# A recommendation ranker on one core: the gathered rows of a tile in groups of 4, 3, 3, 3 chunks instead of 4, 3, 4, 2

## The reference

```python
x0 = emb[ids].reshape(B, -1)
x = x0
for i in range(3):
    x = x0 * (x @ cross_w[i])[:, None] + cross_b[i] + x
h = relu(x0 @ w1 + b1)            # 1664 -> 1024
h = relu(h @ w2 + b2)             # 1024 -> 512
h = relu(h @ w3 + b3)             # 512 -> 256
y = sigmoid(concat([x, h], 1) @ out_w + out_b)
```

## Time and profile before

| | us |
|---|---|
| median of 3 runs | 531.18 |
| the profiled execution | 530.56 |
| its span, first to last instruction | 528.8 |
| PE matmul busy | 480.8 (91%) |
| POOL busy | 379.6 (72%) |
| DVE busy | 186.4 (35%) |
| ACT busy | 84.7 (16%), its DMA issues not counted |

### The profile page before, as it was taken

The page is one execution under the profiler, slowest core; times in us unless marked ns, Lnnn a source line. Parts: engine busy times, 40 slices in busy tenths (PEclk is TensorE's granted clock), DMA queues, the critical chain, the costliest instruction groups (busy, mean ns, idle before and its releaser), DMA issues.

```text
span 528.8 us, 11324 instructions
## 1 busy us (share of the span) xinstructions
PE 480.8 (91%) x2912; PEld 442.2 (84%) x2912; DVE 186.4 (35%) x391; ACT 84.7 (16%) x159; POOL 379.6 (72%) x407
## 2 busy tenths in 40 slices
PE   2699899899999989899898989999899898999997
PEld 1399698898989889798887988888898888989996
DVE  5766414232142423224242321424232142423325
ACT  4642111111011111102011110101111010101111
POOL 5777776777777777777777777777777777777720
PEclk9999999999999999999999999999999999999999
DMA  7971111111111111111111111111111111111100
GB/s 234 387 263 29 28 29 27 28 29 27 29 29 29 28 28 30 29 29 29 27 29 26 30 27 30 26 30 29 26 30 25 30 27 28 27 28 28 28 10 2
DMA packets 19700, 24.90 MB, mean 47 GB/s; under 512 B 9305, under 2 KB 10292, under 8 KB 19636
## 3 DMA queue, kind: packets, MB, share of 16 engines
q0 software_dynamic: 12800, 13.13, 11.2%
q1 hardware_dynamic: 4770, 10.74, 5.7%
q10 hardware_dynamic: 2066, 0.31, 0.3%
HBM read 24.41 MB, written 0.01 MB: 46 GB/s over the span
## 4 chain that ended last, share of the span: by engine, by line
PE 55%; POOL 14%; issue 10%; ACTq 9%; DMA 5%; DVE 4%; ACT 3%; POOLq 0%; DVEq 0%
PE l_bank L717 41%; POOL x_raw L347 14%; ACTq L387 8%; DMA x_raw<-in_L_rec_emb,idx 4%; PE x_bank L717 4%; PE x_bank L729 4%; PE h_bank L771 3%; ACT xT_hi L400 2%; DVE x_raw L516 2%; ACTq L384 1%; PE l_bank L802 1%; DVE xT_lo L523 1%; PE h_bank L741 1%; DVE h2T_lo L528 1%; ACT h2T_hi L411 1%
## 5 line engine op out<-in xcount | busy, mean ns | idle before, releaser
L347 POOL DMA_INDIRECT x_raw<-in_L_rec_emb,idx x400 | 378.8, 947 | 125.5 <-issue 107.7
L717 PE MATMUL l_bank<-w_hi,xT_hi 128*128 128x342 f32 (+1 forms) x624 | 144.9, 333 | 3.5 <-DVE xT_lo L523 3.3
L717 PE MATMUL l_bank<-w_lo,xT_hi 128*128 128x342 f32 (+1 forms) x624 | 137.9, 321 | 0.0
L717 PE MATMUL l_bank<-w_hi,xT_lo 128*128 128x342 f32 (+1 forms) x624 | 137.7, 321 | 0.0
L717 PEld LDWEIGHTS l_bank<-w_hi,xT_hi 128*128 128x128 f32 x624 | 104.0, 191 | 7.9 <-DVE xT_lo L523 5.6
L717 PEld LDWEIGHTS l_bank<-w_lo,xT_hi 128*128 128x128 f32 x624 | 106.8, 191 | 0.0
L717 PEld LDWEIGHTS l_bank<-w_hi,xT_lo 128*128 128x128 f32 x624 | 106.3, 190 | 0.0
L523 DVE TENSOR_TENSOR xT_lo<-x_bank,xT_hi 128x512 fp32r<-128x512 f32 (+1 forms) x66 | 38.2, 578 | 158.5 <-ACT xT_hi L400 158.5
L400 ACT ACTIVATE xT_hi<-x_bank 128x512 fp32r<-128x512 f32 (+1 forms) x66 | 33.5, 507 | 270.3 <-PE x_bank L729 220.4
L729 PE MATMUL x_bank<-identity,x_raw 128*128 128x128 f32 x208 | 34.7, 279 | 27.0 <-DVE x_raw L516 27.0
L729 PEld LDWEIGHTS x_bank<-identity,x_raw 128*128 128x128 f32 x208 | 25.0, 142 | 36.7 <-issue 31.0
(11 more groups left out here) (94 smaller groups left out, 296.5 us busy)
## 6 DMA issues: line engine op xcount, KB each, us to landing
ids<-in_L_rec_emb SPq DMA_DIRECT2D x1152, 0.2 KB
ids<-in_L_rec_emb ACTq DMA_DIRECT2D x896, 0.2 KB
w_raw<-in_L_rec_w SPq DMA_DIRECT2D x18, 512.0 KB, 15.0
x_raw<-in_L_rec_emb,idx POOLq DMA_INDIRECT x400, 2.4
b_rows<-in_L_rec_b SPq DMA_DIRECT2D x1, 512.0 KB
b_rows<-in_L_rec_b SPq DMA_DIRECT2D x1, 256.0 KB
ids<-in_r_ids SPq DMA_DIRECT2D x1, 208.0 KB, 2.7
b_rows<-in_L_rec_b SPq DMA_DIRECT2D x1, 128.0 KB
```

The costliest lines, as they stand in the source:

```text
L347: pool.indirect_dma_start(out=dst, out_offset=None, in_=emb, in_offset=rows).then_inc(landed, 16)
L717: done = pe.matmul(bank[:, 0:b - a], x[:, k, :], w[:, k, a:b], start=(k == 0 and n == 0), stop=(k == last_k and n == 2))
```

## The change

Groups 2 and 3 of tiles 0 to 14 become chunks 7 to 9 and 10 to 12.

```diff
-    SIZES = [4, 3, 4, 2]
+    SIZES = [4, 3, 3, 3]
```

## The result

The changed kernel takes 539.26 us (538.27 to 539.73, 4 runs) against 531.19 us: a ratio of 1.0154, 95% interval 1.0134 to 1.0175. That is slower by 8.1 us where 3.9 were forecast, and outside the range that ended at 537.5. The profiled execution took 539.73 us, its span 537.9.

What follows compares the result with a forecast made beforehand. POOL's gathers and ACT's queue were taken to set PE's pace. Tile 0 +3.3, tile 1 +0.1, tiles 2 to 13 +0.1 and tile 14 +0.4 sum to +3.9 us: median 535.1 us, range 532.6 to 537.5.

Steps and rivals of the forecast that it cites:

- What bounds the kernel: Whole kernel: POOL's gathers and ACT's queue set PE's pace; whatever delays PE up to T(2, 0) delays POOL for good.
- Tile 0, +3.3: Tile 0: PE waits for DVE's splits before T(0, 3) and chunk 10, +3.46 us, less 0.12 for T(0, 2).
- Tiles 1 to 14, +0.6: Later tiles: +0.1 us in tile 1, +0.1 in tiles 2 to 13 together, +0.4 in tile 14.
- Chunks 10 to 12 take 3 x 1.42 = 4.26: Each later tile: the three chunks behind the new wait run at 1.42 us each, 4.26 us.
- 12.13 - 0.11: Tiles 2 to 13: time from x_hi of group 1 to group 3, 12.13 us before, 0.11 less with 384 columns.
- the 5.70 of T(13, 2): Tile 13 before the change: four chunks behind the wait took 5.70 us, read as still 1.42 each.
- The gathers: Late tiles: POOL, 3.4 us late from tile 2 on, and ACT bind about together at the end.
- POOL instead of ACT: Late tiles: ACT's issuing costs less than read, PE catches up with POOL; median 533.4 us, chance 0.15.
- The slow clock: Tile 0: the two chunks behind the waits take 2.17 us, not 1.42; +1.5 more, 536.6 us, chance 0.05.
- Not slower: Tile 0 costs nothing, so POOL isn't delayed and late tiles gain; 530.4 us, chance 0.10.

Runs made afterwards that it cites:

- e1: Changed kernel with make_whole(0, 3) moved up to after split 14 and x_lo(0, 3) to after split 15: 534.88 us, ratio 1.0083.
- e9: Changed kernel with ACT's shares 8, 12, 4, 12, 12, 16, DVE's places in tile 0 left as they are: 530.87 us, ratio 1.0019.
- e6: e1 with four of ACT's DMAs taken from the fetch ahead of x_hi(t, 2), shares 8, 12, 4, 12, 12, 16: 527.18 us, ratio 0.9940.
- e5: e1 with four of ACT's DMAs moved from the fetch ahead of x_hi(t, 3) to the one behind it: 529.15 us, ratio 0.9973.
- e2: Changed kernel with ACT's shares 11, 12, 4, 13, 10, 14 instead of 8, 12, 4, 16, 12, 12: 607.04 us, ratio 1.1415.
- e11: e6 with shares 8, 12, 4, 14, 10, 16, two of them no multiples of four: 543.91 us in its one run.
- e4: Kernel before the change with ACT's shares 11, 12, 4, 13, 10, 14: 604.80 us, ratio 1.1389.
- e10: Changed kernel with only make_whole(0, 3) moved up to after split 14, x_lo(0, 3) still after split 16: 537.31 us, ratio 1.0136.
- e3: e1 with ACT's shares 11, 12, 4, 13, 10, 14: 603.50 us, ratio 1.1359.
- e8: e1 with the transposes of group 3 put back behind chunk 8 in tiles 1 to 13: 534.83 us, ratio 1.0070.

## Why the prediction was right and wrong

- *What bounds the kernel: right.* POOL and ACT's queue are the two, and whatever holds T(2, 0) holds POOL: 4.6 us late in the changed kernel, 0.4 in e1.
- *Tile 0, +3.3: right in mechanism, a little short.* `make_whole` to transposes took 0.72 and `x_lo` to PE 0.60, as was said, and the waits were 1.73 and 1.62. Two small terms were mis-sized: three transposes after a wait take 0.52, not 0.33 (45.93 to 46.45), and the chunk behind the second wait takes 1.69, not 1.42. The stretch lost 3.9 us where the sum had 3.46. T(0, 2) gave back 0.26, not 0.12, so that tile 0 lost some 3.7 us. In the runs DVE's places are worth 3.8 to 4.2 us: the ratios of the changed kernel and e1 differ by 0.0071, those of e9 and e6 by 0.0079.
- *Tiles 1 to 14, +0.6: wrong, and this is the step that failed.* e1 puts them at 4.7 us. The mechanism was right: the gathers' wait goes, ACT's takes its place, and the wait before chunk 10 is there in every tile. The terms that were mis-sized are "Chunks 10 to 12 take 3 x 1.42 = 4.26" (they take 4.51) and "12.13 - 0.11" for the two fetches (12.08 measured, mean of twelve). Per tile that is 0.25 + 0.06 = 0.31: 30.96 forecast, 31.27 measured. So the slower start of PE behind a wait was put at nothing. Fourteen tiles at 0.25 make 3.5 us, twelve at 0.06 make 0.7, and with the 0.6 of the forecast that gives 4.8. The price of the restart stood in the rows of before: the two chunks behind a wait took 3.10, not 2.84. The prediction took the opposite from the 5.70 of T(13, 2), but there the three transposes stand between the wait and the chunks and bear the price themselves, 0.52 instead of 0.33. The same price, paid at chunk 7, is why PE waits 0.46 us before chunk 10 and not 0.7.
- *The gathers: right that they don't hold the late tiles, by more than forecast.* POOL and ACT were to bind about together at the end. But a tile takes 31.27 us, no less than POOL's 31.25, so PE never catches up with POOL, and now and then POOL waits for PE instead. It is 6.0 us late at field 24 of tile 13 (449.56 against 443.56), not 3.4. The low rival, "POOL instead of ACT", is what e5 and e6 made happen by easing ACT's queue.
- *The slow clock.* It came in the profiled execution, 1.6 us on half of layer 2 (4.61 against 3.04), at a place that the rival didn't name. The Trainium skill (TensorE: Matmul & The Clock Gate, "What's actually happening") has the clock fall when TensorE idles. The trace agrees as to the fall (0.51 from 60 to 62 us), and e9, with the same waits and 3.06, shows that it need not come.
- *"Not slower": wrong, and its condition wasn't enough.* It asked only that tile 0 cost nothing, and gave 530.4. e1 met that (its tile 0 ends 0.2 us earlier than before the change) and took 534.88, because ACT's part stayed. e6 removed both.

## What to carry to other kernels

When a group is resized, look for every list elsewhere that was laid out for the old sizes: here two numbers in DVE's order of splits, and the places where ACT issues DMAs. The groups alone made the kernel 1.5% slower; with both fitted to them it is 0.6% faster than before. A wait that comes back in every tile has to be priced with the slower start behind it, and a row of the same instructions right behind a wait gives that price.

## What the runs showed of the hardware

- A register load on ACT's queue is slow when it doesn't start at a multiple of four in its row: 4, 10, 12 and 14 registers took 1.17, 2.42, 2.88 and 3.30 us (e2, e11), where 4, 8, 12 and 16 from such a start took 0.56, 0.73, 0.96 and 1.20 in the kernel before. With four such loads in a tile the kernel was 14% slower (e2 to e4). The Trainium skill (DMA: Bandwidth & Descriptors, "Latency and other measured facts") gives a floor of some 600 ns for such a load and says that the compiler unrolls it by four; the trace agrees roughly: the shortest load of the kernel before, of four registers, took 486 ns, somewhat under that floor, and four registers more added some 0.2 us.
- The first chunk of nine matmuls behind a wait took 1.69 us instead of 1.42, behind a wait of 1.62 us (tile 0); behind one of 0.40 (tile 8), three chunks took 4.51 instead of 4.26, nearly the same price.
- Leaving out the last 2 us of the span, the granted clock fell once in the traces of the changed kernel and of e10, 13 to 16 times in those of e2, e3 and e4, and never in the others. The waits alone don't decide it: e9 has the changed kernel's waits in tile 0, e1 and e8 its waits in the later tiles, and their clock stayed up. Half the runs of e5 list 0.995 or 0.996, so it fell in some of those too.
